# Two absorbed attentions of a fused transformer kernel: fp32 output products in float16 parts

## The reference, cut to what matters

```python
def _L2_xattn_ref(hidden_q, kv_c, Wq, w_kc_q, w_kc_kv, W_qr, W_kr, Wo):
    q_hk = (hidden_q @ Wq.T).reshape(b, s, H, K)              # H = 16 heads, K = 128
    q_big = jnp.einsum('bshk,hkq->bshq', q_hk, w_kc_q)
    kv_rope = kv_c * cos[None] + _rotate_half(kv_c) * sin[None]
    q_r = jnp.einsum('bshq,hqr->bhsr', q_big, W_qr)
    k_r = jnp.einsum('bld,hdr->bhlr', kv_rope, W_kr)
    scores = jnp.einsum('bhsr,bhlr->bhsl', q_r, k_r)
    attn = jax.nn.softmax(scores, axis=-1)                    # 64 keys per head
    ctx_c = jnp.einsum('bhsl,bld->bhsd', attn, kv_rope)
    ctx_lat = jnp.einsum('bhsd,hkd->bshk', ctx_c, w_kc_kv)
    return ctx_lat.reshape(b, s, H * K) @ Wo.T
```

## Time and profile before

| what | value |
|---|---|
| median of 3 runs | 1292.81 us (1286.8 to 1296.47) |
| the profiled execution, its own time | 1289.97 us |
| its span, first to last instruction | 1288.1 us |
| mean granted TensorE clock | 0.979 of full speed |
| PE busy | 1187.8 us, 92% of the span |
| DVE busy | 878.0 us, 68% |
| ACT busy | 509.2 us, 40% |
| POOL busy | 377.6 us, 29% |

### The profile page before, as it was taken

How to read it: one execution, slowest core, us unless ns; L and a number is a source line. 1 busy time by engine, 2 the same in 40 slices (tenths; PEclk the granted TensorE clock), 3 DMA queues, 4 the chain that set the end, 5 groups by cost and what they waited for, 6 DMA issues and landing times.

```text
span 1288.1 us, 21896 instructions
## 1 busy us (share of the span) xinstructions
PE 1187.8 (92%) x8466; PEld 772.8 (60%) x8483; DVE 878.0 (68%) x1713; ACT 509.2 (40%) x1141; POOL 377.6 (29%) x393
## 2 busy tenths in 40 slices
PE   6889999999789999999899888989999888899997
PEld 3654558999545556655566545554556555465565
DVE  3777967667366666666757687887666666766666
ACT  3423360111124344334353235753343353555553
POOL 1540216565203333333203320001333342233332
PEclk9898999999889999999999999999999989999999
DMA  4030140000145444444330000001543200333442
GB/s 145 2 155 21 48 157 23 1 2 2 47 152 132 122 115 115 115 115 119 106 139 1 1 17 2 2 2 34 139 116 119 83 18 2 89 115 115 121 130 83
DMA packets 41544, 97.20 MB, mean 75 GB/s; under 512 B 5446, under 2 KB 18246, under 8 KB 39392
## 3 DMA queue, kind: packets, MB, share of 16 engines
q1 hardware_dynamic: 41440, 95.79, 24.8%
HBM read 94.35 MB, written 1.42 MB: 74 GB/s over the span
## 4 chain that ended last, share of the span: by engine, by line
PE 73%; DVE 16%; ACT 4%; issue 3%; POOL 2%; DMA 1%; SPq 0%; DVEq 0%; POOLq 0%; ACTq 0%
PE PS L1404 10%; PE PS L1405 10%; PE PS L1406 10%; PE PS L1449 4%; PE PS L1451 4%; PE PS L1450 4%; PE PS L1039 3%; PE PS L1057 2%; PE PS L1223 2%; ACT arena L2200 2%; PE PS L1025 2%; PE PS L1027 2%; PE PS L1026 2%; PE PS L2123 1%; DVE small L550 1%
## 5 line engine op out<-in xcount | busy, mean ns | idle before, releaser
L1625 POOL TENSOR_TENSOR arena<-arena,m_g 128x512 f32<-128x512 f32 x142 | 183.1, 1291 | 412.0 <-DMA m_g<-gate_rows 244.0
L1404 PE MATMUL PS<-arena 128*128 128x512 f16 x608 | 231.2, 380 | 2.8 <-DVE arena L1560 2.8
L1405 PE MATMUL PS<-arena 128*128 128x512 f16 x608 | 231.0, 380 | 0.0
L1406 PE MATMUL PS<-arena 128*128 128x512 f16 x608 | 230.8, 380 | 0.0
L1449 PE MATMUL PS<-arena 128*128 128x256 f16 x608 | 165.8, 273 | 11.0 <-DVE arena L1580 8.3
L1451 PE MATMUL PS<-arena 128*128 128x256 f16 x608 | 165.7, 273 | 0.0
L1450 PE MATMUL PS<-arena 128*128 128x256 f16 x608 | 165.7, 273 | 0.0
L1520 ACT ACTIVATE arena<-PS 128x512 f32<-128x512 f32 x112 | 66.9, 597 | 244.5 <-PE PS L1406 234.1
L1563 DVE SCALAR_TENSOR_TENSOR arena<-arena,PS 128x512 f32<-128x512 f32 x112 | 77.0, 687 | 124.7 <-ACT arena L1520 124.3
L1580 DVE TENSOR_TENSOR arena<-arena 128x512 f16<-128x512 f32 x142 | 110.1, 776 | 3.6 <-ACT arena L1530 3.6
L1406 PEld LDWEIGHTS PS<-arena 128*128 128x128 f16 x608 | 59.6, 98 | 72.2 <-issue 0.8
(11 more groups left out here) (282 smaller groups left out, 2256.9 us busy)
## 6 DMA issues: line engine op xcount, KB each, us to landing
w_stage<-in_up SPq DMA_DIRECT2D x80, 256.0 KB, 2.9
m_g<-gate_rows SPq DMA_DIRECT2D x70, 256.0 KB, 4.2
arena<-in_heads SPq DMA_DIRECT2D x16, 1088.0 KB, 5.3
w_stage<-in_down SPq DMA_DIRECT2D x80, 128.0 KB, 4.0
m_g<-gate_rows SPq DMA_DIRECT2D x17, 512.0 KB, 3.9
m_g<-gate_rows SPq DMA_DIRECT2D x6, 448.0 KB, 4.1
m_g<-gate_rows SPq DMA_DIRECT2D x6, 384.0 KB, 4.5
m_g<-gate_rows SPq DMA_DIRECT2D x6, 320.0 KB, 4.1
```

What stands on the lines that cost most here:

```text
L1404: pe.matmul(to, w_hi, x_hi, start=(k == 0), stop=False)
L1405: pe.matmul(to, w_lo, x_hi, start=False, stop=False)
L1406: ins = pe.matmul(to, w_hi, x_lo, start=False, stop=(k == KT - 1))
L1625: pool.tensor_tensor(m_c[:, st % 2, :], m_b[:, st % LAG, :], m_g[:, st // 2 % 2, st % 2, :], ALU.mult).then_inc(s.c, 1)
```

## The change

Probabilities and folded values are kept as float16 high and low parts, and `output` becomes three float16 matmuls per head pair in place of one fp32 one. The high parts are ScalarE's (the old copy, with a scale of 64). The low parts of probabilities and of the even batches' values are VectorE's, from PSUM. For the odd batches' values ScalarE writes one more copy, in fp32, to `f_stage`, and GpSimd subtracts. In the plain attention the sum over 64 keys is done by GpSimd down to 16 (`halved`, two adds) and by VectorE from there, `summed(n)` stands one step later on VectorE, and TensorE's transposes and outputs one step later too. The semaphore `rr` is dropped in favour of `r` in two other stages; no instruction goes with it.

```diff
@@ new functions for both folds @@
+        def pool_values_low(n, q):
+            pool.wait_ge(s.f, 2 * q + 1)
+            pool.tensor_tensor(f[:, 1, 1::2, q, :], f_stage[n].rearrange("p (b c) -> p b c", b=2), f[:, 0, 1::2, q, :],
+                               ALU.subtract).then_inc(norm.pn, 1)
+        def act_values(n, q, c):
+            ps = PS[:, f_banks(n, q)[c], :].rearrange("p (b c) -> p b c", b=2)
+            ins = act.activation(f[:, 0, c::2, q, :], ps, ACT.Copy, scale=SPLIT)
+            if c:
+                if q:
+                    act.wait_ge(norm.pn, norms_before[n] - PAIRS + q)
+                act.activation(f_stage[n], PS[:, f_banks(n, q)[c], :], ACT.Copy, scale=SPLIT).then_inc(s.f, 1)
+        def dve_values_low(n, q):
+            dve.wait_ge(s.f, 2 * q + 1)
+            dve.scalar_tensor_tensor(f[:, 1, 0::2, q, :], PS[:, f_banks(n, q)[0], :].rearrange("p (b c) -> p b c", b=2), SPLIT,
+                                     f[:, 0, 0::2, q, :], ALU.mult, ALU.subtract).then_inc(s.f, 1)
@@ dve_fold1 (dve_fold2 alike: at the end of each q) @@
                 if 0 <= q - 3 < NT // 2:
                     turned(q - 3)
+                dve_values_low(1, q - 1)
             placed(PAIRS - 1)
+            dve_values_low(1, PAIRS - 1)
@@ pe_folded, before pe_rotated @@
+                pe.wait_ge(norm.pn, norms_before[1])
@@ pe_rotated @@
                 if b or e:
-                    pe.wait_ge(soft.t, ROT_0 + 4 * b + e)
+                    pe.wait_ge(soft.low, 4 * b + e)
@@ output, in both attentions @@
-                    ins = pe.matmul(PS[:, out_bank(b, q), 0:D], at_pt[:, q, j * P:(j + 1) * P], fold_f[:, b, j, :], ...)
+                    pe.matmul(to, p_hi, f_hi, start=(j == 0), stop=False)
+                    pe.matmul(to, p_hi, f_lo, start=False, stop=False)
+                    ins = pe.matmul(to, p_lo, f_hi, start=False, stop=(j == PAIRS - 1))
@@ dve_rotated @@
+            def low(b, e):
+                dve.wait_ge(soft.t, ROT_0 + 4 * b + e + 1)
+                dve.scalar_tensor_tensor(lo, PS[:, 6, :], SPLIT, hi, ALU.mult, ALU.subtract).then_inc(soft.low, 1)
+            def lows(g):
+                for e in range(4):
+                    if at_turn(g, TURN_AT[e] + 1) is not None:
+                        low(at_turn(g, TURN_AT[e] + 1), e)
             for g in range(ROT_END):
+                if g < UNITS:
+                    lows(g)
                 if g < UNITS:
                     rotated(g)
...
+                if g >= UNITS:
+                    lows(g)
@@ pe_plain @@
-                if 2 <= n < 4 * B + 2:
-                    transposed(n - 2)
-                if n >= 3:
-                    output(n - 3)
+                if 3 <= n < 4 * B + 3:
+                    transposed(n - 3)
+                if n >= 4:
+                    output(n - 4)
@@ pool_plain @@
+            def halved(n):
+                pool.wait_ge(soft.p, PLAIN_0 + n + 1)
...
+                me.link(pool, pool.tensor_tensor(plain_half_sum, p[:, :, 0:L // 2], p[:, :, L // 2:L], ALU.add))
...
+                pool.tensor_tensor(plain_quarter[:, n % 4, :, :], plain_half_sum[:, :, 0:L // 4], plain_half_sum[:, :, L // 4:L // 2],
+                                   ALU.add).then_inc(s.halved, 1)
+            for n in range(4 * B + 1):
+                if n:
+                    normalised(n - 1)
+                if n < 4 * B:
+                    halved(n)
@@ dve_plain @@
+            for n in range(1, 4 * B + 5):
+                if 4 <= n < 4 * B + 4:
+                    low(n - 4)
                 if n < 4 * B:
                     softened(n)
-                    summed(n)
-                if n >= 6 and n % 4 >= 2:
-                    added((n - 6) // 4, n % 2)
+                if n <= 4 * B:
+                    summed(n - 1)
+                if n >= 7 and n % 4 in (0, 3):
+                    added((n - 7) // 4, (n - 7) % 4)
```

More of the change, by code:

```diff
@@ L180, in build @@
         plain_p, _ = take(8192, [2, 1024])
-        plain_pt = [take(a, [1024])[0] for a in (10240, 18432)]
+        plain_pt = [take(a, [2, 1024], F16)[0] for a in (10240, 18432)]
         plain_x, _ = take(16384, [2, KT, NT, P], F16)
+        plain_half_sum, _ = take(20992, [8, L // 2])
+        plain_quarter, _ = take(21504, [4, 8, L // 4])
+        f_stage = {1: xT[:, 0, 0:4, :].rearrange("p t c -> p (t c)"), 2: plain_p[:, 1, 512:1024]}
         e_pair, _ = take(20992, [D])
@@ L641, in pool_folded @@
                         pool.wait_ge(ln.xn, 3 * NT)
+                        pool_values_low(1, 0)
                     pool.memset(fold_m[:, quad, :, :, :, :].rearrange("p t f b c -> p (t f b c)"), 0.0).then_inc(s.zero, 1)
+                for q in range(1, PAIRS):
+                    pool_values_low(1, q)
                 pool_rotated()
@@ L646, in pool_folded @@
                 pool_ln(2 * n)
+                for q in range(PAIRS):
+                    pool_values_low(2, q)
                 pool_plain()
@@ L1052, in output @@
             def output(b, q):
-                pe.wait_ge(soft.t, ROT_0 + 4 * b + 2 + q + 1)
+                pe.wait_ge(soft.low, 4 * b + 2 + q + 1)
                 if b or q:
@@ L1156, in added @@
                 tile = x[:, QT * b + q, :]
-                dve.tensor_tensor(tile, tile, PS[:, out_bank(b, q), 0:D], ALU.add).then_inc(soft.x, 1)
+                dve.scalar_tensor_tensor(tile, PS[:, out_bank(b, q), 0:D], UNSPLIT, tile, ALU.mult, ALU.add).then_inc(soft.x, 1)
                 dve_stats(3, QT * b + q)
+            def low(b, e):
+                half, q = EVENTS[e]
+                hi, lo = (rot_pt[:, q, a, half * 512:(half + 1) * 512] for a in range(2))
+                dve.wait_ge(soft.t, ROT_0 + 4 * b + e + 1)
[4 more added lines that the diff above has]
+                        low(at_turn(g, TURN_AT[e] + 1), e)
             for g in range(ROT_END):
+                if g < UNITS:
+                    lows(g)
                 if g < UNITS:
@@ L1206, in transposed @@
                 if n >= 2:
-                    pe.wait_ge(soft.t, PLAIN_0 + n - 1)
+                    pe.wait_ge(soft.low, PLAIN_LOW_0 + n - 1)
                 else:
@@ L1250, in evacuated, with normalised @@
                     act.wait_ge(soft.y_ps, 2 * NT + QT * (b - 1) + q + 1)
-                act.activation(plain_pt[q][:, half * 512:(half + 1) * 512], PS[:, n % 2, :], ACT.Copy).then_inc(soft.t, 1)
+                act.activation(plain_pt[q][:, 0, half * 512:(half + 1) * 512], PS[:, n % 2, :], ACT.Copy, scale=SPLIT).then_inc(soft.t, 1)
             act_keys_high(PAIRS - 1)
-            for n in range(4 * B + 2):
+            for n in range(4 * B + 3):
+                if n >= 3:
+                    evacuated(n - 3)
                 if n < 4 * B:
                     exponential(n)
-                if n >= 2:
-                    evacuated(n - 2)
         def pool_plain():
-            pool = nc.gpsimd
-            for n in range(4 * B):
+            pool, s, me = nc.gpsimd, att[2], own["pool"]
+            def halved(n):
+                b, half, q = plain_event(n)
+                p = plain_half(q, half).rearrange("p (h l) -> p h l", l=L)
+                pool.wait_ge(soft.p, PLAIN_0 + n + 1)
+                if n:
+                    pool.wait_ge(s.halved, n)
+                me.link(pool, pool.tensor_tensor(plain_half_sum, p[:, :, 0:L // 2], p[:, :, L // 2:L], ALU.add))
+                if n >= 4:
+                    pool.wait_ge(soft.sums, PLAIN_0 + n - 3)
+                pool.tensor_tensor(plain_quarter[:, n % 4, :, :], plain_half_sum[:, :, 0:L // 4], plain_half_sum[:, :, L // 4:L // 2],
+                                   ALU.add).then_inc(s.halved, 1)
+            def normalised(n):
                 b, half, q = plain_event(n)
@@ L1284, in summed @@
                 total, inverse = (small[:, q, a, 8 * half:8 * half + 8] for a in (1, 2))
-                dve.wait_ge(soft.p, PLAIN_0 + n + 1)
-                me.link(dve, dve.tensor_reduce(total, plain_half(q, half).rearrange("p (h l) -> p h l", l=L), AX.X, ALU.add))
+                dve.wait_ge(s.halved, n + 1)
+                me.link(dve, dve.tensor_reduce(total, plain_quarter[:, n % 4, :, :], AX.X, ALU.add))
                 dve.reciprocal(inverse, total).then_inc(soft.sums, 1)
@@ L1291, in added, with low @@
                 tile = x[:, QT * b + q, :]
-                dve.tensor_tensor(tile, tile, PS[:, (5, 7)[q], 0:D], ALU.add).then_inc(soft.x, 1)
+                dve.scalar_tensor_tensor(tile, PS[:, (5, 7)[q], 0:D], UNSPLIT, tile, ALU.mult, ALU.add).then_inc(soft.x, 1)
                 dve_stats(5, QT * b + q)
+            def low(n):
+                b, half, q = plain_event(n)
+                hi, lo = (plain_pt[q][:, a, half * 512:(half + 1) * 512] for a in range(2))
+                dve.wait_ge(soft.t, PLAIN_0 + n + 1)
+                dve.scalar_tensor_tensor(lo, PS[:, n % 2, :], SPLIT, hi, ALU.mult, ALU.subtract).then_inc(soft.low, 1)
             softened(0)
```

(12 more changed lines are left out.)

61 lines of the change are left out of this document (38 added, 23 removed).

## The result

The changed kernel takes 1299.68 us in the median of 20 runs (1292.25 to 1307.77), the kernel before 1294.22 (20 runs, the three of the table above among them); the ratio is 1.0046, 95% interval 1.003 to 1.0062, so 4 to 8 us slower. The forecast was 1295.0, within 1285 to 1304 and "within 1%". The profiled execution took 1297.46 us with a span of 1295.7 (before: 1289.97 and 1288.1).

The account below looks back on a forecast made before the run. The prediction took TensorE as the bound in all four touched stages; its terms, 6.7 + 1.5 - 2.5 + 0.3 - 3.7 = +2.3 us on a median of 1292.8, gave 1295.1, say 1295.0, range 1285 to 1304.

Parts of the forecast that it names:

- TensorE's saving: Both attentions: shorter outputs save 6.7 us in the rotated and 6.7 in the plain one, 13.4 at most before waits.
- Rival C: In the attentions' output product: float16 is no faster, all costs stay, 1308 us; chance 0.03.
- Fold 1: Layer 1's fold: extra copies, low parts and subtraction make TensorE wait, 6.7 us lost (3 to 8).
- pairs with turned rows: In fold 1: keys wait for VectorE's low part, 5.9 us per pair in place of 4.98, 3.6 over four pairs.
- Rival A: In the folds: TensorE's other work hides the extra work, kernel 4 to 9 us faster, 1286; chance 0.22.
- The clock at the handover: From fold 1's last keys to the first rotated queries: these queries run at 1.2 GHz, 1.5 us lost (0 to 2.3).
- Rotated attention: Layer 1's attention: 6.7 us saved, 2.1 lost to late low parts in three batches, 2.1 in the tail; net -2.5.
- Fold 2: Layer 2's fold: TensorE's work hides the extra work except perhaps in the first two pairs, +0.3 us (0 to 3).
- Plain attention: Layer 2's attention: VectorE and GpSimd loop of 3.06 us per event, level with TensorE; -3.7 us (0 to -6.7).
- The sum: Whole kernel: 6.7 + 1.5 - 2.5 + 0.3 - 3.7 = +2.3 us, waits giving back what TensorE saves.
- Rival B: Clock falls at handover, plain pipeline's filling and rotated tail, 1300 us; or plain loop of 3.46 or more, +3.7; chance 0.22.

Follow-up runs that it names:

- evac_first: Changed kernel with ScalarE's copy of turned probabilities ahead of the exponential in the rotated attention; 1297.5 us, ratio 1.0035 to the kernel before.
- low_first: Changed kernel with VectorE's low part of the even batches' values ahead of that of the turned rows in fold 1; 1296.65 us, ratio 1.0019.
- dve_odd: Changed kernel with the odd batches' low parts by VectorE in both folds, without ScalarE's fp32 copy and GpSimd's subtraction; 1300.85 us, ratio 1.0067.
- both_orders: Changed kernel with the order swaps of low_first and evac_first together, no idle matmuls; 1293.56 us, ratio 1.0001 to the kernel before.
- combo: both_orders plus idle matmuls ahead of fold 1's last keys, ahead of the first rotated query and in layer 2's self-attention; 1288.72 us, ratio 0.9942.
- plain_warm: Kernel before with only the change's fold 2 and plain attention, plus seven idle matmuls in layer 2's self-attention; 1287.58 us, ratio 0.9948.

## Why the prediction was right in its class and short in its size

**TensorE's saving, 13.4 us.** The batch of 33.62 us in evac_first shows the rotated part of it (1.74 where 1.68 was expected). Rival C is out. The plain part can't be seen in full, since that stage is no longer PE's.

**Fold 1, +6.7.** 50.4 - 44.2 = 6.2 in the profiles in which the clock costs nothing there. Term by term: pairs with turned rows 5.77 where I said 5.9, with the named cause confirmed by low_first; the first pairs 0.04 longer in all where I said 0.2; last keys 4.62 after those before, 1.22 more than 3.40 where I said 1.25; first query 5.24 after them at full clock, 1.72 more than 3.52 where I said 1.65. Rival A, that PE's spare work fills these waits, is refuted.

**The clock at the handover, +1.5 (0 to 2.3).** The changed kernel's profile lost 2.7: 1.4 in fold 1 (5.24 against 6.61) and 1.3 in the rotated queries. The second part is what I counted, and it comes out near 1.5 in every profile without idle matmuls (1.0 to 1.3). The first I left out: the keys and values between the two gaps at half clock (1.95 and 1.57 for 1.08 and 1.07 in the rows above). It is a term of its own, but of this execution and dve_odd's; in five of seven profiles it is nothing. The Trainium skill, "TensorE: Matmul & The Clock Gate", section "HAM oscillation", has the work behind each stall starting at half rate. By it the work between the two gaps was to be charged as well; the rows agree for the first queries in all seven profiles and for the keys or values between the gaps in only two. So this term was of the right size in most executions and 1.2 short in the one that was compared.

**Rotated attention, -2.5.** With the clock held 150.8 - 153.2 = -2.4. The kernel before shows 153.2 in its own profile and 154.1 in three other executions of the same code, so -3.3 by those. The stall of 0.8 per batch where I said 0.7 is the one that I derived from the earlier trace rows. From the first to the last query the stage went from 130.0 to 127.4 us with the clock held: six shorter outputs (-5.0) and three stalls (+2.4) are -2.6. In the tail PE's waits for GpSimd's last `normalised`, for ScalarE's copies before and for VectorE's low parts after grew from 2.9 + 1.6 to 3.4 + 3.3 us, 2.2 more where I said 2.1 (0.5 and 1.7, where I said 1.4 and 0.7). In the same tail the granted clock is 0.50 between 334 and 338 us before (0.59 in the next two), and between 338 and 346 (0.54 in the next two) in the changed kernel.

**Fold 2, +0.3.** 41.6 in both profiles; nothing.

**Plain attention, -3.7 (0 to -6.7).** -4.7 in the changed kernel's profile (61.9 to 57.2), but -3.2 to -3.6 (58.3 to 58.7) in five of the others that have this half, where the clock of the stretch was 0.97. The loop with GpSimd is the bound in the steady part, at 2.90 us in the early events and 2.96 to 3.10 later, 2.99 in the mean where I said 3.06. (The steps with `added` were put at 3.17; the parts named for them add up to 3.19 to 3.29. It changes nothing.)

**The sum.** The four stages of the two profiles give +7.5 - 0.3 + 0 - 4.7 = +2.5 where I said +2.3. That the two agree to 0.2 is luck: fold 1 came out 0.8 over its term and the rotated attention with its first queries' clock 0.7 over, fold 2 0.3 and the plain attention 1.0 under, and in other executions fold 1 is 1.4 us shorter, the plain attention up to 1.5 longer and fold 2 up to 4.8 longer. The medians differ by 5.5. The difference of 3 is in no stage of the change, and a forecast built from its stages had no term for it. It stays open. Part of it may be chance (the interval is 4 to 8 us, and the time ahead of fold 1's first folding alone, in unchanged code, is 145.9 to 152.4 us in the fourteen profiles). Part may be clock: 15 of the 20 runs of the changed kernel have a mean granted clock of 0.966 to 0.969 over the whole span, the median of the 105 runs of the kernel before beside the experiments is 0.975 (0.979 in its profiled execution), and the two fastest of the changed kernel, 1292.25 and 1293.38, have 0.975 and 0.974. But both_orders has 0.963 to 0.969 in all its runs and is as fast as the kernel before, so a lower mean clock isn't by itself lost time.

Rival B named the mechanism, half clock behind gaps; of its three places the handover is one in every profile without idle matmuls, the rotated tail is at 0.50 for longer than before though its gap grew to 3.4 us and not to 4.5, and the plain pipeline's filling is at 1.00 in this profile and at 0.53 to 0.95 in others (combo, plain_warm). A fourth, 50 us behind the change, was in neither the forecast nor a rival, and either kernel meets it. What decides that a given run meets it is open. B's time, 1300, is nearer to the measured 1299.68 than the forecast's 1295.0; its sum of places is not what the rows show.

## What to carry to other kernels

Splitting a product to make TensorE faster moves its work to the engines that prepare the parts. Read, before anything else, where in each engine's order the new instruction stands: two swaps of order, which cost nothing, gave back all of the 5.5 us. Charge every new gap of PE with the work behind it at half clock, take the work between two gaps as a risk on top (1.4 us here, in one profile of seven), and fill the gap with idle matmuls where a bank is free. And before a difference of two profiles is given to the change or to a repair, look at the same place in the profiles of the other versions, and put the same repair into the kernel before too.

## What was unexpected of the hardware

The clock is worth as much here as the change. Seven idle matmuls in one gap of 1.6 us took 4.0 us off the kernel before and 5.0 off the changed one. Of the fourteen profiled executions, the nine in which this gap of the self-attention was empty show a stretch behind it of 22.5, 23.4, 23.5, 25.6, 28.2 (four times) and 28.3 us, the five with the gap filled 21.8 or 21.9 in each. Fold 2 behaves likewise: 40.0 or 41.6 us with the old code, 41.6 to 41.9 or 46.3 to 46.4 with the new, the granted clock between 630 and 640 us being 1.00, 0.83 to 0.88, and 0.52 to 0.55.

GpSimd's subtraction with float16 output took 1.154 us where its multiplication of the same 128x512 elements in fp32 took 1.042; VectorE's with a PSUM operand took 0.686.
